# Tokenizer: two of four pairs of attention-weight chunks spread by DMA inside SBUF, two by TensorE products

## The reference, cut to what matters

```
x = features.reshape(b, c, h, s, w, s)                      # s = 4: 16x16 windows of 16 pixels
reduce_feats = x.mean((3, 5)).reshape(b, c, hw).transpose(0, 2, 1)
unf = ...                                                    # (b, 256 windows, 16 pixels, 64 channels)
q = _ln(reduce_feats, ln_q_w, ln_q_b) @ Wq.T                 # one query per window, 8 heads of 8 channels
kv = _ln(unf, ln_kv_w, ln_kv_b) @ Wkv.T                      # a key and a value per pixel
attn = softmax(einsum('bhpd,bhpnd->bhpn', q * scale, k))     # over the 16 pixels of a window
aggre = einsum('bhpn,bhpnd->bhpd', attn, v)
return reduce_feats + aggre @ proj_w.T + proj_b
```

## Time and profile before

| | |
|---|---|
| runs shown | 656.38, 654.85, 656.12 us; median 656.12 |
| profiled execution | 657.6 us, span 655.6 us |
| TensorE busy | 609.2 us (93%) |
| VectorE busy | 549.3 us (84%) |
| GpSimd busy | 462.4 us (71%) |
| ScalarE busy | 459.8 us (70%) |
| granted TensorE clock, mean | 0.976 |

### The profile page before, as it was taken

The page is one execution under the profiler, slowest core; times in us unless marked ns, Lnnn a source line. Parts: engine busy times, 40 slices in busy tenths (PEclk is TensorE's granted clock), DMA queues, the critical chain, the costliest instruction groups (busy, mean ns, idle before and its releaser), DMA issues. The chain is left out here.

```text
span 655.6 us, 16806 instructions
## 1 busy us (share of the span) xinstructions
PE 609.2 (93%) x5402; PEld 333.0 (51%) x5402; DVE 549.3 (84%) x996; ACT 459.8 (70%) x931; POOL 462.4 (71%) x449
## 2 busy tenths in 40 slices
PE   1899999999999999998779999998699999999995
PEld 1222333333333333332245666665389998989894
DVE  4589999999999999998656999998898888888882
ACT  0797787777777777874248888887466776677663
POOL 5756889898988898855670366666787766666666
PEclk9999999999999999999779999999789999999998
DMA  7233333332222333000007975111231222222210
GB/s 283 112 129 130 129 129 129 129 123 87 82 108 119 129 131 128 20 1 14 0 21 129 141 152 180 39 36 43 62 92 57 75 68 60 63 56 56 57 33 1
DMA packets 49213, 57.94 MB, mean 88 GB/s; under 512 B 31934, under 2 KB 44710, under 8 KB 46906
## 3 DMA queue, kind: packets, MB, share of 16 engines
q1 hardware_dynamic: 43738, 48.02, 24.4%
q0 software_dynamic: 5120, 6.99, 3.3%
q10 hardware_dynamic: 288, 2.10, 0.9%
HBM read 50.03 MB, written 10.28 MB: 92 GB/s over the span
## 5 line engine op out<-in xcount | busy, mean ns | idle before, releaser
L2061 POOL DMA_INDIRECT out<-orow,m_rows x96 | 109.0, 1135 | 49.8 <-ACT orow L1999 27.2
L825 PE MATMUL s_proj<-x_px,w_kv 64*64 64x512 f32 x256 | 130.8, 603 | 0.0
L822 PE MATMUL s_proj<-x_px,w_kv 64*64 64x512 f32 x256 | 130.1, 600 | 0.1
L1933 DVE TENSOR_TENSOR m_xs<-m_rows 128x768 f32<-128x768 f32 x96 | 91.4, 953 | 20.0 <-PE s_proj L2023 12.7
L1203 POOL DMA_INDIRECT rows_by_group<-r_pay,r_slot_i x64 | 68.1, 1064 | 42.0 <-DVE r_slot_i L1532 8.4
L487 POOL TENSOR_TENSOR half_px<-x_px 128x1024 f32<-128x1024 f32 x30 | 71.6, 2387 | 35.4 <-DMA x_px<-in_x 35.4
L508 POOL TENSOR_TENSOR pre<-va 128x1024 f32<-128x1024 f32 x32 | 76.1, 2379 | 26.4 <-DVE va L608 24.7
L590 DVE TENSOR_TENSOR qk<-s_proj,q 128x512 f32<-128x512 f32 x128 | 85.5, 679 | 7.9 <-PE s_proj L825 5.6
L313 ACT ACTIVATE x_sq<-x_px 128x1024 f32<-128x1024 f32 x64 | 67.1, 1048 | 33.4 <-PE b_x L877 19.2
L608 DVE TENSOR_TENSOR va<-b_a,v_sb 128x1024 f32<-128x1024 f32 x64 | 78.1, 1220 | 8.6 <-PE b_a L842 8.6
L2041 PE MATMUL s_logits<-m_xsT,m_w_cur 128*64 128x128 f32 x1344 | 84.0, 276 | 0.0
(11 more groups left out here) (307 smaller groups left out, 1735.2 us busy)
## 6 DMA issues: line engine op xcount, KB each, us to landing
x_px<-in_x SPq DMA_DIRECT2D x15, 2048.0 KB, 7.9
m_rows<-rows_by_group SPq DMA_DIRECT2D x96, 72.0 KB, 1.8
wt<-in_w2T SPq DMA_DIRECT2D x8, 512.0 KB
rows_by_group<-rows_by_group SPq DMA_DIRECT2D x1, 2286.0 KB, 9.4
x_px<-in_x ACTq DMA_DIRECT2D x2, 1024.0 KB, 6.6
out<-orow,m_rows POOLq DMA_INDIRECT x96, 2.5
rows_by_group<-r_pay,r_slot_i POOLq DMA_INDIRECT x64
wt<-in_w2T SPq DMA_DIRECT2D x2, 256.0 KB
```

The costliest lines, as they stand in the source:

```text
L822: mm(b_k[i][LO, :], w_kv[LO, 0, LO], px(t, j, LO), start=True, stop=True)
L825: mm(b_k[i][HI, :], w_kv[HI, 0, HI], px(t, j, HI), start=True, stop=True).then_inc(done["kv_product"], 1)
L1933: d.tensor_tensor(xs[:, i % RING, :, :], rows[:, i, X0:X0 + C].rearrange("p (o c) -> p o c", o=1).broadcast_to([P, UNITS, C]), rows[:, i, ...
L2061: nc.gpsimd.indirect_dma_start(out_d, bass.IndirectOffsetOnAxis(ap=rows[:, i, ID0:ID0 + 1].bitcast(I32), axis=0), orow[:, i, :], None, bou ...
```

## The change

The spreading of pairs 2 and 3 is taken from TensorE in every tile but the last. SyncE issues for each of them four transfers from a_sb to a new tile a_far, in SBUF: 8 rows (the heads of one chunk of one image) to 64 rows, each row eight times, 512 elements wide. These are issued between the loads of x, in SyncE's order. va_mul reads a_far in place of the bank for these pairs. The buffer of GpSimd's pixel sums, half_px, has half its size and is used by both halves in turn.

```diff
-    half_px = sb("half_px", [P, TH, 2, HW])
+    half_px = sb("half_px", [P, TH // 2, 2, HW])
+    a_far = sb("a_far", [P, 2, 2, CH])
+    far_in = [sem(f"far_in{i}") for i in range(2)]
+    FAR_LOADS = 16 * 4
+    def near(t):
+        return 4 if t == TILES - 1 else 2
@@ SyncE
-        for t in range(NX, TILES):
+        def next_tile(t):
+            if not live(t):
+                return
             (the waits and the load of x as before)
+        def spread_far(t, i):
+            if t > 0:
+                sp.wait_ge(done["va_ready"], 4 * (t - 1) + 3 + i)
+            for e in range(2):
+                j = ORDER[4 + 2 * i + e]
+                for b in range(2):
+                    heads = a_sb[16 * j + HEADS * b:16 * j + HEADS * b + HEADS, :]
+                    sp.dma_start(a_far[half(1 - b), i, e, :], heads.rearrange("q (o n) -> q o n", o=1).broadcast_to([HEADS, HD, CH])).then_inc(far_in[i], 16)
+        next_tile(NX)
+        for t in range(TILES - 1):
+            sp.wait_ge(done["weights"], 2 * t + 2)
+            for i in range(2):
+                spread_far(t, i)
+            next_tile(t + NX + 1)
@@ GpSimd, halve and quarter
-            if t > 1:
-                pool.wait_ge(done["px_quartered"], 2 * (t - 2) + h + 1)
-            g.tensor_tensor(half_px[:, s, :, :], v[:, s, 0:2, :], ...
+            if 2 * (t - 1) + h > 0:
+                pool.wait_ge(done["px_quartered"], 2 * (t - 1) + h)
+            g.tensor_tensor(half_px[:, :, :, :], v[:, s, 0:2, :], ...
@@ VectorE, va_mul
-            v.wait_ge(done["a_spread"], 4 * t + i + 1)
+            if i < near(t):
+                v.wait_ge(done["a_spread"], 2 * t + i + 1)
+            else:
+                v.wait_ge(far_in[i - 2], FAR_LOADS * (t + 1))
-            d.tensor_tensor(va[:, at:at + 3:2, :], b_a[:, :, :], v_sb[:, t % 2, n:n + 2, :], ...
+            spread = b_a[:, :, :] if i < near(t) else a_far[:, i - 2, :, :]
+            d.tensor_tensor(va[:, at:at + 3:2, :], spread, v_sb[:, t % 2, n:n + 2, :], ...
@@ VectorE, weigh
-                v.wait_ge(done["a_spread"], 4 * t)
+                v.wait_ge(done["a_spread"], 2 * t)
+                for i in range(2):
+                    v.wait_ge(far_in[i], FAR_LOADS * t)
@@ TensorE, spread
-            if not live(t):
+            if not live(t) or i >= near(t):
                 return
-            m = 4 * t + i
-            if m > 0:
-                pe.wait_ge(done["va_ready"], m)
+            if i > 0:
+                pe.wait_ge(done["va_ready"], 4 * t + i)
+            elif t > 0:
+                pe.wait_ge(done["va_ready"], 4 * t - 2)
```

More of the change, by code:

```diff
@@ L484, in halve @@
             s = slice(H2 * h, H2 * h + H2)
-            if t > 1:
-                pool.wait_ge(done["px_quartered"], 2 * (t - 2) + h + 1)
-            g.tensor_tensor(half_px[:, s, :, :], v[:, s, 0:2, :], v[:, s, 2:4, :], ALU.add).then_inc(done["px_halved"], 1)
+            if 2 * (t - 1) + h > 0:
+                pool.wait_ge(done["px_quartered"], 2 * (t - 1) + h)
+            g.tensor_tensor(half_px[:, :, :, :], v[:, s, 0:2, :], v[:, s, 2:4, :], ALU.add).then_inc(done["px_halved"], 1)
         def quarter(t, h):
@@ L496, in quarter @@
                 pool.wait_ge(done["pooled"], t)
-            g.tensor_tensor(quarter_px[:, s, :], half_px[:, s, 0, :], half_px[:, s, 1, :], ALU.add).then_inc(done["px_quartered"], 1)
+            g.tensor_tensor(quarter_px[:, s, :], half_px[:, :, 0, :], half_px[:, :, 1, :], ALU.add).then_inc(done["px_quartered"], 1)
         def fold_rows(t, e):
@@ L607, in va_mul @@
             at = slot(n)
-            d.tensor_tensor(va[:, at:at + 3:2, :], b_a[:, :, :], v_sb[:, t % 2, n:n + 2, :], ALU.mult).then_inc(done["va_ready"], 1)
+            spread = b_a[:, :, :] if i < near(t) else a_far[:, i - 2, :, :]
+            d.tensor_tensor(va[:, at:at + 3:2, :], spread, v_sb[:, t % 2, n:n + 2, :], ALU.mult).then_inc(done["va_ready"], 1)
         def kv_var(t):
@@ L832, in spread @@
                 pe.wait_ge(done["weights"], 2 * t + 2)
-            m = 4 * t + i
-            if m == 0:
+            if t == 0 and i == 0:
                 pe.wait_ge(folded, SWAPPED)
-            if m > 0:
-                pe.wait_ge(done["va_ready"], m)
+            if i > 0:
+                pe.wait_ge(done["va_ready"], 4 * t + i)
+            elif t > 0:
+                pe.wait_ge(done["va_ready"], 4 * t - 2)
             lo, hi = ORDER[2 * i], ORDER[2 * i + 1]
```

## The result

The changed kernel takes 681.28 us (678.95 to 683.25, 4 runs) beside 656.25 us (654.85 to 656.64, 4 runs) for the kernel before in the same session: a ratio of 1.0381, interval 1.0360 to 1.0401. The forecast was 685, slower; the range was 663 to 703. Direction and size held, the size partly by luck: of the sum's terms one was too large, one was put at nothing and one was missing, and they nearly cancelled.

What follows compares the result with a forecast made beforehand. The prediction took a loop through VectorE and TensorE, 18.15 us a tile, as the bound. Exclusion at 12 x 2.15 = 25.8 us plus 3, together +29, took 657.6 to 686.4, shown as 685; range 663 to 703.

Steps and rivals of the forecast that it cites:

- The bound: Tile loop, 18.15 us: VectorE from scaling to addition, TensorE from square sums to second scores; fewer spreads gain under 1 us.
- The rival that counted on TensorE's order: Square sums: no exclusion, TensorE's order starts them, up to 0.86 us a tile gained, period 17.3, 645 us; chance 6%.
- The exclusion: Pairs 2 and 3: VectorE products with two SBUF inputs and GpSimd's SBUF sums wait for each other, 2.15 us a tile.
- The transfers: SyncE's queue: eight 128 KB transfers a tile, 0.33 to 0.6 us an issue, next x load 0 to 1 us later; nothing.
- The sum: Whole kernel: 25.8 us for twelve tiles plus 3 for tiles 12 to 14, together +29, giving 685 us; chance 62%.
- What would show it: Signs in the profile after: a_far products at 2 to 3 us, longer GpSimd sums, TensorE waits of over 2 us.
- Loads 20.3 apart: Sign in the tile loop: x loads 20.3 us apart, the predicted period in place of 18.15.

Runs made afterwards that it cites:

- run 1: The kernel before with the spread products of pairs 2 and 3 left out and no transfers: 656.16 us, ratio 0.9996.
- run 7: The kernel before without spreads of pairs 2 and 3, VectorE's addition moved ahead of pair 3's product, TensorE's output product ahead of projection 3: ratio 0.9967.
- run 2: The changed kernel without its transfers, a_far filled once with a constant, so pairs 2 and 3 still read SBUF: 682.16 us, ratio 1.0391.
- run 3: The changed kernel with all transfers, but products of pairs 2 and 3 read PSUM in place of v: 663.47 us, ratio 1.0114.
- run 4: The kernel before with the change's transfers, SyncE order and halved half_px added; a_far is written and not read: 664.91 us, ratio 1.0119.
- run 11: The kernel before with the change's transfers added, unread, each from 64 different rows: 680.67 us beside 680.08 for the kernel before.
- run 5: The changed kernel with SyncE issuing the load of x after pair 2's transfers and ahead of pair 3's: 739.11 us, ratio 1.0904.
- run 6: The changed kernel with TensorE still spreading pairs 2 and 3 into PSUM, where nobody reads them: ratio 1.0410.

## Why the prediction was right

- *The bound.* Right. The loop through VectorE was named from three rows, and run 1 measured what leaving the spreads out is worth: nothing (0.9996). The rival that counted on TensorE's order overstated its own price, too: run 7 gives 0.25 us a tile, not up to 0.86, since the weights' wait stands just behind the addition's. The prediction did not look for the second wait.
- *The exclusion.* Right in mechanism, and by itself nearly right in size: forecast 2.15 us a tile and 29 in all; run 2 has a mean period of 20.05 where the forecast had 20.3, 24.8 us of stretch in its products and 25.6 us in time. In the changed kernel the same term is 16.5.
- *The transfers.* This step failed: "I put it at nothing", with issues at 0.33 to 0.6 us and x late by 0 to 1. An issue took 1.28, x went out about 4 us late and landed 3 us later still. Alone that costs 6.9 to 8.3 us (runs 3 and 4), for GpSimd then does enter the loop. The row that the estimate leaned on was a load with another shape of source. The prediction had the eight-row source in view and allowed "some tenths" for it, which it took from no row; run 11 shows 0.7 us on every issue and 3 us on the landing of x.
- *The clock.* The prediction has no term for it. In four tiles a wait of TensorE of 2 to 3 us was followed by a fall of the granted clock, and its part of the loop took 4.9 us more in sum.
- *The sum.* That 685 lies within 4 us of 681.3 is partly luck: the exclusion was forecast 12 us dearer than it was in the changed kernel, and 8 us or so of late load and low clock were at nothing or absent. The effects don't add at full price, either. The stretch of 16.5 and the 6.9 to 8.3 of runs 3 and 4 make 23.4 to 24.8, close to the 25.0 measured, but those two runs have no fall of the clock; in the changed kernel's own trace the late load's direct part is 3.1 us and the clock's 4.9. That x late is what lowered the stretch is argued from the phases (153.87 to 156.2 in the changed kernel is a halving where run 2 has the fold of va); run 5, meant to test it, did not.
- *What would show it.* Far products between 1.22 and 2.57 us: seen, most of them below the "2 to 3" (their mean is 1.77). GpSimd's sums over their own length: seen. Loads 20.3 apart: they are 19.4 to 21.2, mean 20.0. TensorE's waits for VectorE of 2 us, and square sums that start right behind the addition and wait up to 2.2 us for it: seen.

## What to carry to other kernels

Before moving work off a busy engine, follow one iteration and find whose result ends each wait; here a wholly busy TensorE could lose a tenth of its work for nothing, and behind the wait that bound it a second one stood 0.25 us away. Where an operand comes from is part of an instruction's price: a VectorE product with both inputs in SBUF queues against GpSimd's sums, and that was the larger part of the change's cost. An engine that is made to wait can also come back at its lower clock: compare the same stretch of work in several tiles, with the granted clock beside it. Price a transfer from a row with the same shape of source, and then ask which other transfer stands behind it in its queue.

## What was not expected of the hardware

- A transfer of 8 SBUF rows, each read eight times (128 KB), costs 1.28 us of SyncE when others are in flight, 0.60 at its shortest; the same bytes from 64 rows 0.60, landing in 2.3 us. The Trainium skill (DMA: Bandwidth & Descriptors, Why a DMA increments its semaphore by 16 and not by 1) has a rule that would fit, a source whose outer size is 8 uses 8 of the 16 engines. The traces agree as far as they can: the 16 engines are busy 0.45 of the time on average with such transfers one behind the other, and 0.83 with the plain ones. Which engines work they don't show.
- VectorE and GpSimd take turns, in order of arrival: in the changed kernel a product issued into a sum ends 1.1 us after that sum, and the sum behind is then held until the product is done (2.25 for 1.28). With one input in PSUM neither is touched (run 3).
- TensorE's granted clock fell to 0.50, the lower of its two levels (1.2 GHz), four times in the changed kernel's tokenizer, each time within 1.2 us of the end of an idle time (2.90, 2.16, 1.97 and 2.92 us long); another idle time of 2.18 us, up to 263.7 us, had no fall behind it. It cost time although TensorE had waited just before: 4.9 us in four tiles, and 3.5 in the two falls of run 6.
